# Blocks without tokens skipped and spread over the expert pairs, and all shared-expert units placed before the expert loop

## The chip, the cores and the metric

One core of one Trainium2 chip runs the whole kernel. The time is device microseconds of one execution, from the first to the last instruction; lower is better. TensorE (PE), VectorE (DVE), ScalarE (ACT), GpSimd (POOL) and SyncE (SP) each run their own instruction list in order and meet only at semaphores; SP, ACT and POOL also issue DMA transfers, each on a queue of its own (q1, q10 and q0 in the profile).

## The reference

Four layers on x of shape (8, 256, 256), each `x = x + layernorm(layer(layernorm(x)))`: softmax attention with 16 heads, a mixture of experts, an mLSTM layer with 8 heads, and a gated feed-forward layer with 2:4 sparsity. The change concerns the second:

```python
_, topk_idx = jax.lax.top_k(logits + router_bias, K)          # 64 experts, K = 4, 2048 tokens
combine = jnp.zeros((n, E), x.dtype).at[jnp.arange(n)[:, None], topk_idx].add(topk_scores)
g = jnp.einsum('nd,edf->enf', flat, Wg)
u = jnp.einsum('nd,edf->enf', flat, Wu)
h = jax.nn.silu(g) * u
out = jnp.einsum('enf,efd->nd', h * combine.T[:, :, None], Wd)
for i in range(Sg.shape[0]):                                  # 2 shared experts, 256 wide each
    sh = jax.nn.silu(flat @ Sg[i]) * (flat @ Su[i])
    out = out + sh @ Sd[i]
```

## The kernel before, in words

**Attention** (to about 290 us of the profile). For each of the 8 batches the normed input of the expert layer is stored to the DRAM tensor `xnd`, on SP's queue.

**Shared experts and router** (about 290 to 357 us). The two shared experts are cut into 16 units: unit n is token group n // 4 (512 tokens) and weight block n % 4. A unit is `gate(n)`, `up(n)` on PE (12 matmuls of 512 columns), a Silu on ACT (`hidden_gate`), a product on DVE, a rounded copy on ACT (`hidden_high`), the rest of it by a subtraction on POOL (`low_hidden`), and `down_unit(n)` on PE (12 matmuls of 256 columns), which PE issues two units later. After four units ACT copies the group's rows out (`shared_rows`) and SP stores them to `shd`. The constant `AHEAD` says how many units stand ahead of the expert loop: 12 of 16. Between them DVE computes the router's choice (`router_step(n)` after unit n's product): the number of blocks of 128 tokens that each expert needs, the table `ebrow` of the expert of each block, and the token numbers in each block, `rows_at`. For the last, DVE writes 0/1 marks for four token tiles at a time (`mark_rows(c)`, c = 0 to 3), ACT multiplies them by the token's number (`token_marks(c)`), PE contracts them (`block_rows(c)`, 16 matmuls), and DVE copies the sum out (semaphore `r_inv`).

**The expert loop** (about 357 to 580 us). There are always 128 blocks, in 64 pairs; pair i is blocks 2i and 2i+1. Tokens of one expert fill whole blocks and a partly filled last one; blocks behind the last used one have no tokens, and take expert 63. From the inputs and the reference's routing 96 blocks are used, with 8192 filled places in all, so that blocks 96 to 127, the pairs 48 to 63, are empty. For each pair:
- SP reads each block's expert number and loads its weights, 192 KB a block, into one of 7 slots (`expert_weights`).
- POOL issues two indirect gathers of token rows from `xnd` (L529) into one of 4 slots; a place without a token transfers nothing. It waits until PE has transposed pair i-4.
- PE transposes the rows (L1298), ACT copies them (L782), PE multiplies gate and up (L1310), ACT takes the Silu (L798), DVE the product (L1999), PE multiplies down (L1321), DVE copies the result (L2006), and ACT issues the store of 256 KB to `yd` (L787). PE's order is: transposes of i+1, gate and up of i, down of i-1.

During pairs 8 to 23 DVE also does one step each of the combine weights (`weight_step`).

**After the loop** PE runs the units 12 to 15. Meanwhile POOL waits for all stores of the loop and fetches batch 0's expert rows from `yd` (`gathers(0)`, 8 indirect gathers, L545), DVE sums them (L1962), adds, and norms twice (L1566); with that PE starts the mLSTM layer (L938). SP stores the last shared rows and then loads the first half of the feed-forward weights, 1.5 MB. The mLSTM layer and the feed-forward layer follow, to 1017.7 us.

Of the kernel before, what the change touches and what calls it, by code (L numbers as in the profile page):

```python
# [15 lines left out]
P = 128  # L16
# [10 lines left out]
NJ = NSH  # L27
NQ = NUNIT
AHEAD = (NQ - 1) * NJ
# [25 lines left out]
def build(nc, io, out):  # L55
    ctx = ExitStack()
    with ctx:
# [31 lines left out]
        ebrow = sb("ebrow", [1, XB], mybir.dt.int32)  # L89
# [202 lines left out]
        def sums(b):  # L292
# [17 lines left out]
            x_st r_zero r_oh r_im r_inv sh_o0 sh_o1 e_xt e_xc e_gu e_sg e_h e_dn e_y e_w0 e_w1 e_w2 e_w3 e_x0 e_x1 e_x2 e_x3  # L310
# [23 lines left out]
        def pair_weights(i):  # L334

            n = i % WRING
            return raw[:, n, :] if n < RING else more_weights[n - RING]

# [30 lines left out]
        def _(sp):  # L369
# [19 lines left out]
            for b in range(NB):  # L389
                sp.wait_ge(s["a_xn2"], b + 1)  # L390
                sp.dma_start(xnd[b * T:(b + 1) * T, :].rearrange("(t p) d -> p t d", p=P),
                             xn_all[:, 2 * b:2 * b + 2, :]).then_inc(s["x_st"], 16)

# [6 lines left out]
            def expert_weights(i):  # L400
# [11 lines left out]
            sp.wait_ge(s["r_eb"], 1)  # L412
            for i in range(RING):
                expert_weights(i)
# [26 lines left out]
        def _(pool):  # L441
# [83 lines left out]
            for i in range(XPAIR):  # L525
                if i >= RING:
                    pool.wait_ge(s["e_xt"], i - RING + 1)
                for b in range(2):
                    pool.indirect_dma_start(xg[:, i % RING, b, :], None, xnd[:],  # L529
                                            bass.IndirectOffsetOnAxis(ap=rows_at[:, 2 * i + b:2 * i + b + 1], axis=0),  # L530
                                            bounds_check=NT * P - 1, oob_is_err=False
                                            ).then_inc(s[f"e_x{i % RING}"], 16)
            for k in range(RING):
                pool.wait_ge(s[f"e_o{k}"], 16 * (XPAIR // RING))
# [45 lines left out]

            pool.wait_ge(s["r_w"], 1)
# [47 lines left out]
        def _(act):  # L629
# [132 lines left out]
            for n in range(1, AHEAD):  # L762
# [27 lines left out]
            act.wait_ge(s["r_inv"], 1)  # L790
            expert_inputs(0)
# [11 lines left out]

            for n in range(AHEAD, NQ * NJ):
                hidden_unit(n)
            shared_rows(3)
# [127 lines left out]
        def _(pe):  # L934
# [331 lines left out]
            for n in range(2, AHEAD):  # L1266
# [12 lines left out]
                if n == 11:  # L1279
                    block_rows(0)  # L1280
# [46 lines left out]
            pe.wait_ge(s["f_rows"], 2 * (NQ - 1))  # L1327
# [14 lines left out]
            for n in range(AHEAD, NQ * NJ):  # L1342
                gate(n)
                up(n)
                if n >= AHEAD + 2:
                    down_unit(n - 2)
            down_unit(NQ * NJ - 2)
            down_unit(NQ * NJ - 1)
            pe.wait_ge(s["f_rows"], 2 * NQ)
# [200 lines left out]
        def _(dve):  # L1550
# [326 lines left out]
            def block_table():  # L1877
                dve.wait_ge(s["r_ebT"], 1)
                dve.tensor_copy(ebrow[:], S[3][0:1, 0:XB]).then_inc(s["r_eb"], 1)
# [6 lines left out]
            def router_step(n):  # L1886
# [36 lines left out]
                if n == 11:  # L1923
                    for c in range(1, 4):
                        mark_rows(c)
# [67 lines left out]
            for i in range(XPAIR + 1):  # L1993
# [8 lines left out]
                if i:  # L2002
                    dve.wait_ge(s["e_dn"], i)
                    if i - 1 >= RING:
                        dve.wait_ge(s[f"e_o{(i - 1) % RING}"], 16 * ((i - 1) // RING))
# [7 lines left out]
            for n in range(AHEAD, NQ * NJ):  # L2013
                product(n)
# [326 lines left out]
```

## Time and profile before

| | |
|---|---|
| three timed runs, us | 979.53, 972.15, 970.7 (median 972.15) |
| profiled execution, span | 1017.7 us |
| PE busy | 862.2 us, 85% |
| DVE, ACT, POOL busy | 667.7, 389.5, 396.7 us |
| DMA | 77.66 MB, mean 76 GB/s |
| loads and stores | q1 (SP) 40.92 MB, q10 (ACT: the stores to `yd`) 16.78 MB, q0 (POOL) 18.92 MB |

The page gives the span and what each engine did in it. The span belongs to the one profiled execution, and is 45.5 us longer than the median of the timed runs. Idle time stands ahead of the instruction that had to wait, with the engine or transfer that released it; "issue" means that the profile shows nothing it waited for, "remote" and "another core or an unknown queue" that it shows no releaser.

### The profile page before, as it was taken

The page shows a single profiled execution, that of the slowest core. Times are in us where ns is not written, and L with a number is a line of the kernel's source. Part 1 is how long each engine was busy: PE and PEld are TensorE (multiplying, and loading weights), DVE is VectorE, ACT ScalarE, POOL GpSimd, SP SyncE. Part 2 cuts the span into 40 slices and gives each one's busy share as a digit, 9 for nine tenths or more (in the row PEclk, how much of TensorE's full clock was granted, in tenths as well). Part 3 has the DMA queues.
Part 4 walks back from the last instruction along what each step waited for, and adds up shares of the span by engine and source line. Part 5 has one row for each costly group of instructions (what it writes and reads, how often), then busy time and mean ns, then how long its engine had stood idle before and what let it go on. Part 6 is the DMA issues. An engine that isn't in the chain of part 4 may idle for free.

```text
span 1017.7 us, 18542 instructions
## 1 busy us (share of the span) xinstructions
PE 862.2 (85%) x6718; PEld 722.4 (71%) x6718; DVE 667.7 (66%) x1500; ACT 389.5 (38%) x764; POOL 396.7 (39%) x548
## 2 busy tenths in 40 slices
PE   4899899898688857667777859899999999999994
PEld 3777777776576846556666748778788888788883
DVE  6567777765577615885444547668778865867875
ACT  2244444444433713232222325435555564222220
POOL 3123333323432266766565283466665322100001
PEclk9799999998899968998898977758888887999997
DMA  7000000000000248888876551221111000000001
GB/s 248 2 1 13 12 12 9 5 12 12 22 1 22 87 136 260 250 257 242 242 222 184 162 178 52 82 59 52 46 42 41 0 1 1 0 1 21 22 1 41
DMA packets 59384, 77.66 MB, mean 76 GB/s; under 512 B 9746, under 2 KB 51997, under 8 KB 59304
## 3 DMA queue, kind: packets, MB, share of 16 engines
q1 hardware_dynamic: 32040, 40.92, 13.1%
q0 software_dynamic: 9856, 18.92, 6.9%
q10 hardware_dynamic: 17408, 16.78, 4.7%
q8 instruction: 47, 0.77, 0.3%
q14 instruction: 33, 0.27, 0.1%
HBM read 61.88 MB, written 23.07 MB: 83 GB/s over the span
## 4 chain that ended last, share of the span: by engine, by line
PE 43%; DVE 12%; issue 5%; another core or an unknown queue 4%; ACT 3%; POOL 2%; DMA 1%; ACTq 0%; POOLq 0%; DVEq 0%
PE S L1310 5%; PE S L1298 4%; PE S L959 3%; PE S L961 3%; PE S L960 3%; PE S L944 3%; PE ZO L1518 2%; PE ZO L1321 2%; PE T L1321 2%; PE T L1518 2%; PE ZO L1431 2%; DVE work L1566 1%; PE ZO L1433 1%; PE ZO L1432 1%
## 5 line engine op out<-in xcount | busy, mean ns | idle before, releaser
L529 POOL DMA_INDIRECT work<-xnd,rows_at x128 | 134.8, 1053 | 87.6 <-issue 38.6
L446 POOL TENSOR_SCALAR veps<-mv 128x2 f32<-128x2 f32 (+1 forms) x63 | 15.6, 247 | 287.8 <-DVE mv L1561 287.6
L1999 DVE TENSOR_TENSOR work<-work,S 64x256 f32<-64x256 f32 x128 | 54.2, 424 | 83.0 <-ACT work L798 52.9
L455 POOL TENSOR_SCALAR_AFFINE_SELECT work<-work 128x256 f32<-128x256 f32 x128 | 53.7, 444 | 118.0 <-ACT work L650 118.0
L959 PE MATMUL ZO<-parts 128*128 128x256 f32 x224 | 71.4, 319 | 16.6 <-DVE parts L1600 6.4
L959 PE MATMUL S<-xr,parts 128*128 128x512 f32 x192 | 83.5, 435 | 0.8 <-issue 0.8
L960 PE MATMUL S<-xr,parts 128*128 128x512 f32 x192 | 77.5, 404 | 0.0
L961 PE MATMUL S<-xr,parts 128*128 128x512 f32 x192 | 77.5, 403 | 0.0
L782 ACT ACTIVATE work<-S 128x512 f32<-128x512 f32 x64 | 38.2, 597 | 100.7 <-PE S L1298 43.5
L650 ACT ACTIVATE work<-S 128x768 f32<-128x768 f32 x64 | 51.7, 812 | 55.5 <-PE S L1033 55.5
L960 PE MATMUL ZO<-parts 128*128 128x256 f32 x224 | 66.3, 296 | 0.0
L961 PE MATMUL ZO<-parts 128*128 128x256 f32 x224 | 66.2, 295 | 0.0
L1033 PE MATMUL S<-parts 32*128 32x256 f32 (+1 forms) x768 | 57.9, 288 | 4.8 <-DVE parts L1626 3.8
L959 PEld LDWEIGHTS ZO<-parts 128*128 128x128 f32 x224 | 45.3, 202 | 21.9 <-issue 9.3
L1310 PE MATMUL S<-work,raw 128*128 128x128 f32 x296 | 46.7, 309 | 10.8 <-issue 10.7
L545 POOL DMA_INDIRECT attn_w<-yd,slots x44 | 49.8, 1131 | 11.9 <-issue 11.9
L1298 PE MATMUL S<-ident,work 128*128 128x128 f32 x256 | 47.4, 314 | 8.2 <-DMA work<-xnd,rows_at 8.2
L1033 PEld LDWEIGHTS S<-parts 32*128 32x128 f32 x768 | 48.9, 191 | 7.1 <-DVE parts L1626 5.0
L1310 PEld LDWEIGHTS S<-work,raw 128*128 128x128 f32 x296 | 42.5, 221 | 13.0 <-issue 12.9
L447 POOL TENSOR_TENSOR rstd<-veps,mhalf 128x2 f32<-128x2 f32 (+1 forms) x63 | 48.1, 763 | 5.2
L798 ACT ACTIVATE work<-S 64x256 f32<-64x256 f32 x64 | 24.1, 377 | 59.1 <-remote 30.8
L960 PEld LDWEIGHTS ZO<-parts 128*128 128x128 f32 x224 | 45.8, 205 | 0.1
(330 smaller groups left out, 2355.7 us busy)
## 6 DMA issues: line engine op xcount, KB each, us to landing
yd<-work ACTq DMA_DIRECT2D x64, 256.0 KB
raw<-in_experts SPq DMA_DIRECT2D x74, 192.0 KB
work<-in_experts SPq DMA_DIRECT2D x36, 192.0 KB
lg_all<-in_experts SPq DMA_DIRECT2D x18, 192.0 KB
xnd<-attn_w SPq DMA_DIRECT2D x8, 256.0 KB, 2.1
shd<-work SPq DMA_DIRECT2D x8, 256.0 KB, 2.3
work<-xnd,rows_at POOLq DMA_INDIRECT x128
raw<-in_ffn SPq DMA_DIRECT2D x2, 1024.0 KB, 5.4
```

The lines of the kernel that those rows point to most:

```text
L447: pool.tensor_tensor(rstd[:, 0:n], veps[:, 0:n], mhalf[:, 0:n], ALU.pow).then_inc(s["ln_rs"], 1)
L455: last = pool.affine_select(out=diagonal, in_=diagonal, compare_op=ALU.is_ge, fill=0.0, base=0, pattern=[[0, 2], [1, P]], channel_multipli ...
L529: pool.indirect_dma_start(xg[:, i % RING, b, :], None, xnd[:], bass.IndirectOffsetOnAxis(ap=rows_at[:, 2 * i + b:2 * i + b + 1], axis=0), ...
L545: pool.indirect_dma_start(gathered(b, t, k), None, yd[:], bass.IndirectOffsetOnAxis(ap=slots[:, 2 * b + t, k:k + 1], axis=0)).then_inc(s[" ...
L650: act.activation(pt[n % 6], SS[:, at:at + 1024].rearrange("p (r x) -> p r x", r=2)[:, :, 0:384], ACT.Exp).then_inc(s["a_exp"], 1)
L959: pe.matmul(dst, a(0), b(0), start=start, stop=False, skip_group_check=True)
L960: pe.matmul(dst, a(0), b(1), start=False, stop=False, skip_group_check=True)
L961: return pe.matmul(dst, a(1), b(0), start=False, stop=stop, skip_group_check=True)
L1033: return pe.matmul(bank[:, 2 * half * P:(2 + half) * P], side, top, start=k == 0 and half == 0, stop=k == 2, skip_group_check=True)
L1298: last = pe.transpose(S[i % 2][:, o:o + P], xg[:, i % RING, b, c * P:(c + 1) * P], ident[:])
L1310: last = pe.matmul(S[2 + i % 2][:, b * P:(b + 1) * P], pair_weights(i)[:, o:o + P], xT[:, i % 2, b, c, :], start=(c == 0), stop=(c == KC - 1))
L1999: last = dve.tensor_tensor(hx[64 * half:64 * half + 64, i % 2, :], sgx[64:128, i % 2, :], S[2 + i % 2][64:128, 0:256], ALU.mult)
```

## The change

1. Pair i is now blocks i and 64 + (27 i + 13) % 64 (`pair_blocks`). The first is always used; of the second ones 32 are empty, about every second pair.
2. SP's load of a second block's weights (from pair 7 on) and ACT's store of a second block carry a condition, `used > k`, and move nothing if the block is empty; the semaphore is still incremented. `used` is one more element of `ebrow`, read once by SP and once by ACT.
3. The store of a pair is two DMAs of 128 KB in place of one of 256 KB.
4. The upper 64 blocks of `yd` are filled beforehand with the input, 4 DRAM-to-DRAM copies of 2 MB each on SP's queue, behind the first four stores to `xnd` in the attention stage. ACT waits for them before the loop.
5. `AHEAD` is 16: all units stand ahead of the loop, none behind. `mark_rows`, `token_marks` and `block_rows` are spread over units 10 to 14.

```diff
-AHEAD = (NQ - 1) * NJ
+AHEAD = NQ * NJ
+        def pair_blocks(i):
+            return i, XPAIR + (27 * i + 13) % XPAIR
@@ SP
+                if b < 4:
+                    at = XPAIR * P + b * NT * P
+                    sp.dma_start(yd[at:at + NT * P, :], io["x"]).then_inc(s["y_base"], 16)
-                for b in range(2):
-                    e = sp.value_load(ebrow[0:1, 2 * i + b:2 * i + b + 1], min_val=0, max_val=E - 1)
-                    sp.dma_start(pair_weights(i)[:, b * EW:(b + 1) * EW],
-                                 io["experts"][bass.ds(e, 1)].squeeze(0)).then_inc(pair_loaded(i)[0], 16)
+                for b, k in enumerate(pair_blocks(i)):
+                    e = sp.value_load(ebrow[0:1, k:k + 1], min_val=0, max_val=E - 1)
+                    sp.dma_start(pair_weights(i)[:, b * EW:(b + 1) * EW], io["experts"][bass.ds(e, 1)].squeeze(0),
+                                 cond=used > k if b and i >= WRING else None).then_inc(pair_loaded(i)[0], 16)
+            shared_rows(3)
             for i in range(XPAIR):
                 if WRING <= i + WRING - 1 < XPAIR:
                     expert_weights(i + WRING - 1)
-            shared_rows(3)
@@ POOL
-                for b in range(2):
+                for b, k in enumerate(pair_blocks(i)):
                     pool.indirect_dma_start(xg[:, i % RING, b, :], None, xnd[:],
-                                            bass.IndirectOffsetOnAxis(ap=rows_at[:, 2 * i + b:2 * i + b + 1], axis=0),
+                                            bass.IndirectOffsetOnAxis(ap=rows_at[:, k:k + 1], axis=0),
@@ ACT
-                if n in (6, 10):
+                if n in (6, 10, 14):
                     shared_rows((n - 6) // 4)
-                if n == 10:
-                    token_marks(0)
-            for c in range(1, 4):
-                token_marks(c)
-            shared_rows(2)
+                if 10 <= n < 14:
+                    token_marks(n - 10)
+            shared_rows(3)
-                act.dma_start(yd[i * 256:(i + 1) * 256, :].rearrange("(b p) d -> p b d", p=P),
-                              ysb[:, i % RING].rearrange("p b h d -> p b (h d)")).then_inc(s[f"e_o{i % RING}"], 16)
+                for b, k in enumerate(pair_blocks(i)):
+                    act.dma_start(yd[k * P:(k + 1) * P, :], ysb[:, i % RING, b].rearrange("p h d -> p (h d)"),
+                                  cond=used > k if b else None).then_inc(s[f"e_o{i % RING}"], 16)
-            for n in range(AHEAD, NQ * NJ):
-                hidden_unit(n)
-            shared_rows(3)
@@ PE
-                if n == 11:
-                    block_rows(0)
+                if 11 <= n < 15:
+                    block_rows(n - 11)
                 if n >= 2:
                     down_unit(n - 2)
             down_unit(AHEAD - 2)
-            block_rows(1)
             down_unit(AHEAD - 1)
-            block_rows(2)
-            block_rows(3)
@@ DVE
-                if n == 11:
-                    for c in range(1, 4):
-                        mark_rows(c)
+                if 11 <= n < 14:
+                    mark_rows(n - 10)
+                if n == 14:
                     block_rows()
```

PE and DVE lose their loops `for n in range(AHEAD, NQ * NJ)` behind the expert loop in the same way.

**POOL, in front of the gathers.** `parts` is the output of `low_hidden`, `rows_at` the index table of the token gathers. Before:

```order
L466 TENSOR_TENSOR parts<-work,parts 128x512 [waits f_hh] x7
L521 MEMSET work 128x2048 [waits r_mask]
L466 TENSOR_TENSOR parts<-work,parts 128x512 [waits f_hh] x5
L529 DMA work<-xnd,rows_at 128x256 [waits r_inv,x_st,r_zero]
L529 DMA work<-xnd,rows_at 128x256 x7
```

Now:

```order
L474 TENSOR_TENSOR parts<-work,parts 128x512 [waits f_hh] x7
L529 MEMSET work 128x2048 [waits r_mask]
L474 TENSOR_TENSOR parts<-work,parts 128x512 [waits f_hh] x9
L537 DMA work<-xnd,rows_at 128x256 [waits r_inv,x_st,r_zero]
L537 DMA work<-xnd,rows_at 128x256 x7
```

Sixteen of these subtractions, unit 15's among them, stand in front of the first gather where twelve did.

**PE, at the end of the expert loop.** The L1321 rows are the down products of the last two pairs. Before, the first unit of the last token group follows at once (`xr`, `parts` into `S`):

```order
L1321 MATMUL T<-lg_all,work 128x128 [waits e_y,e_h]
L1321 MATMUL T<-lg_all,work 128x128 x3
L1321 MATMUL ZO<-raw,work 128x128 [waits e_y,e_h]
L1321 MATMUL ZO<-raw,work 128x128 x3
L959 MATMUL S<-xr,parts 128x512 [waits f_sg,e_y,e_h]
L960 MATMUL S<-xr,parts 128x512
```

Now the mLSTM layer's first transposes (L945, L938 before) and gate product do:

```order
L1325 MATMUL T<-lg_all,work 128x128 [waits e_y,e_h]
L1325 MATMUL T<-lg_all,work 128x128 x3
L1325 MATMUL ZO<-raw,work 128x128 [waits e_y,e_h]
L1325 MATMUL ZO<-raw,work 128x128 x3
L945 MATMUL T<-ident,work 128x128 [waits c_const,w_c,c_xn,e_y,e_h]
L945 MATMUL T<-ident,work 128x128 x3
L1356 MATMUL T<-work,attn_w 40x256 [waits c_xtc]
```

The 96 matmuls of units 12 to 15 are gone from this place, and the wait for the normed input (`c_xn`) is the next thing that PE meets.

## Rows read from the trace of the kernel before

**Rows 1.** The page: busy time of two engines; shares of the chain that ended last.
```profile
PE 862.2 (85%) x6718; PEld 722.4 (71%) x6718; DVE 667.7 (66%) x1500; ACT 389.5 (38%) x764; POOL 396.7 (39%) x548
...
PE 43%; DVE 12%; issue 5%; another core or an unknown queue 4%; ACT 3%; POOL 2%; DMA 1%; ACTq 0%; POOLq 0%; DVEq 0%
```

**Rows 2.** The chain that ended last, in time: start us, us, what.
```profile
390.81 2.02 another core or an unknown queue
...
550.70 4.24 another core or an unknown queue
```

**Rows 3.** Stretches: us, busy (instructions) of PE, PEld, DVE, ACT, POOL, PEclk, DMA share, GB/s.
```profile
140.00:180.00 40.00, 36.68 (x506) 29.67 (x508) 29.81 (x75) 18.02 (x36) 13.49 (x32) 1.00 0.04 15
...
436.00:456.00 20.00, 13.60 (x122) 11.31 (x122) 16.31 (x26) 5.80 (x13) 13.85 (x13) 1.00 0.84 258
...
519.80:524.00 4.20, 1.28 (x10) 0.97 (x8) 0.00 (x0) 0.51 (x1) 2.43 (x3) 1.00 0.42 126
```

**Rows 4.** Timeline of PE in front of the loop: start us, us, engine, line, instruction, [idle before].
```profile
332.89 0.40 PE L959 MATMUL S<-xr,parts 128*128 128x512 f32 x1
335.69 0.28 PE L959 MATMUL T<-parts 128*128 128x256 f32 x1
337.13 0.40 PE L959 MATMUL S<-xr,parts 128*128 128x512 f32 x1
...
342.26 2.06 PE L1204 MATMUL S<-work 128*128 128x128 f16 x16 [2.18 <-ACT work L757]
344.08 0.43 PE L959 MATMUL T<-parts 128*128 128x256 f32 x1
```

**Rows 5.** The same timeline, from the last `block_rows` to the first transposes.
```profile
354.51 2.06 PE L1204 MATMUL S<-work 128*128 128x128 f16 x16 [0.60 <-ACT work L757]
363.03 1.09 PE L1298 MATMUL S<-ident,work 128*128 128x128 f32 x4 [6.46 <-DMA work<-xnd,rows_at]
```

**Rows 6.** POOL: all `low_hidden` (min/median/max ns), and the first gather of the timeline.
```profile
L466 POOL TENSOR_TENSOR parts<-work,parts x12: 1262/1296/2841, 283.0 to 344.2; 128x512 fp32r<-128x512 f32 x12
```
```profile
357.90 1.29 POOL L529 DMA_INDIRECT work<-xnd,rows_at  x1 [12.20 <-DVE rows_at L1866]
```

**Rows 7.** The token gathers on POOL: duration ns, and what ended the idle time before them.
```profile
L529 POOL DMA_INDIRECT work<-xnd,rows_at x128: 996/1002/2380, 357.9 to 567.1; - x128
...
  issue: 38.6, 105
```

**Rows 8.** Timeline of DVE: copies of the results of pairs 12, 13, 25, 47, 48, 57, 63.
```profile
416.48 0.69 DVE L2006 COPY work<-T 128x512 f32<-128x512 f32 x1
...
419.35 0.69 DVE L2006 COPY work<-ZO 128x512 f32<-128x512 f32 x1
...
458.94 0.69 DVE L2006 COPY work<-ZO 128x512 f32<-128x512 f32 x1
...
534.31 0.69 DVE L2006 COPY work<-ZO 128x512 f32<-128x512 f32 x1 [0.23 <-remote]
...
536.29 0.69 DVE L2006 COPY work<-T 128x512 f32<-128x512 f32 x1
...
569.10 0.69 DVE L2006 COPY work<-ZO 128x512 f32<-128x512 f32 x1 [0.25 <-remote]
...
579.28 0.69 DVE L2006 COPY work<-ZO 128x512 f32<-128x512 f32 x1
```

**Rows 9.** Timelines behind the loop: PE, POOL, DVE, and SP's load of feed-forward weights.
```profile
596.99 0.28 PE L961 MATMUL ZO<-parts 128*128 128x256 f32 x1
...
607.04 1.09 PE L938 MATMUL T<-ident,work 128*128 128x128 f32 x4 [9.77 <-DVE work L1566]
```
```profile
582.83 0.77 POOL L558 DMA_DIRECT2D attn_w<-shd  x1 [14.68 <-issue]
```
```profile
596.37 3.63 DVE L1962 SCALAR_TENSOR_TENSOR attn_w<-attn_w,wtop 128x256 f32<-128x256 f32 x8 [1.25 <-DMA attn_w<-yd,slots]
```
```profile
602.93 0.50 SPq L430 DMA_DIRECT2D raw<-in_ffn  x1
```

More of the change, by code:

```diff
@@ L88, in build @@
         wtop = sb("wtop", [P, NT, TOPK])
-        ebrow = sb("ebrow", [1, XB], mybir.dt.int32)
+        ebrow = sb("ebrow", [1, XB + 1], mybir.dt.int32)
         eye1 = sb("eye1", [P, H1])
@@ L309, in build @@
             f_g f_u f_sg f_h f_hh f_hl f_wh f_wl f_blk f_rows
-            x_st r_zero r_oh r_im r_inv sh_o0 sh_o1 e_xt e_xc e_gu e_sg e_h e_dn e_y e_w0 e_w1 e_w2 e_w3 e_x0 e_x1 e_x2 e_x3
+            x_st y_base r_zero r_oh r_im r_inv sh_o0 sh_o1 e_xt e_xc e_gu e_sg e_h e_dn e_y e_w0 e_w1 e_w2 e_w3 e_x0 e_x1 e_x2 e_x3
             e_o0 e_o1 e_o2 e_o3 m_in m_in1 m_add
@@ L412, in _ @@
             sp.wait_ge(s["r_eb"], 1)
+            used = sp.value_load(ebrow[0:1, XB:XB + 1], min_val=0, max_val=XB)
             for i in range(RING):
@@ L533, in _ @@
             for k in range(RING):
-                pool.wait_ge(s[f"e_o{k}"], 16 * (XPAIR // RING))
+                pool.wait_ge(s[f"e_o{k}"], 32 * (XPAIR // RING))
             base = 3 * NB
@@ L578, in head_event @@
                 pool.tensor_tensor(hv, hv, mhalf[:], ALU.pow).then_inc(s["c_hr"], 1)
+            pool.wait_ge(s["y_base"], 64)
             pool.wait_ge(s["r_w"], 1)
@@ L786, in expert_rows @@
                 act.wait_ge(s["e_y"], i + 1)
-                act.dma_start(yd[i * 256:(i + 1) * 256, :].rearrange("(b p) d -> p b d", p=P),
-                              ysb[:, i % RING].rearrange("p b h d -> p b (h d)")).then_inc(s[f"e_o{i % RING}"], 16)
+                for b, k in enumerate(pair_blocks(i)):
+                    act.dma_start(yd[k * P:(k + 1) * P, :], ysb[:, i % RING, b].rearrange("p h d -> p (h d)"),
+                                  cond=used > k if b else None).then_inc(s[f"e_o{i % RING}"], 16)
             act.wait_ge(s["r_inv"], 1)
+            act.wait_ge(s["r_eb"], 1)
+            act.wait_ge(s["y_base"], 64)
+            used = act.value_load(ebrow[0:1, XB:XB + 1], min_val=0, max_val=XB)
             expert_inputs(0)
@@ L1325, in expert_down @@
                 last.then_inc(s["e_dn"], 1)
-            pe.wait_ge(s["f_rows"], 2 * (NQ - 1))
+            pe.wait_ge(s["f_rows"], 2 * NQ)
             pe.wait_ge(s["f_sg"], AHEAD)
@@ L1341, in _ @@
             pe.wait_ge(s["e_y"], XPAIR)
[L1342 to L1349, printed above, removed]
             pe.wait_ge(s["w_c"], 144)
@@ L1878, in block_table @@
                 dve.wait_ge(s["r_ebT"], 1)
-                dve.tensor_copy(ebrow[:], S[3][0:1, 0:XB]).then_inc(s["r_eb"], 1)
+                dve.tensor_copy(ebrow[0:1, XB:XB + 1], upto[0:1, E - 1:E])
+                dve.tensor_copy(ebrow[0:1, 0:XB], S[3][0:1, 0:XB]).then_inc(s["r_eb"], 1)
             def combine_weights():
@@ L2004, in _ @@
                     if i - 1 >= RING:
-                        dve.wait_ge(s[f"e_o{(i - 1) % RING}"], 16 * ((i - 1) // RING))
+                        dve.wait_ge(s[f"e_o{(i - 1) % RING}"], 32 * ((i - 1) // RING))
                     dve.tensor_copy(ysb[:, (i - 1) % RING].rearrange("p b h d -> p h b d"),
@@ L2012, in _ @@
                     second_constants(i - 24)
-            for n in range(AHEAD, NQ * NJ):
-                product(n)
-                dve.wait_ge(s["f_hh"], n + 1)
-                dve.tensor_tensor(hp[:, n % 4, 1, :], hf[n % 2], hp[:, n % 4, 0, :], ALU.subtract).then_inc(s["f_hl"], 1)
             moe_sum(0, ch)
```

## The prediction

> **What bounds the kernel now.** I read the page first, then the chain of waits in order of time, then stretches by engine, then the timelines of single engines around the three places that the change touches. PE is busy 85% of the span [rows 1], and the chain that ended last runs mostly over it. The exception is the expert loop: in a stretch of it PE works 13.60 of 20 us, POOL 13.85, and the DMA engines are 84% busy at 258 GB/s [rows 3]. From the first gather (357.90) [rows 6] to the end of the last result copy (579.28 + 0.69) [rows 8] it takes 222.1 us.
>
> Part of that is not in what I can explain. The chain of waits has pieces of 2.0 and some 4.3 us whose releaser the trace does not show [rows 2]; nine of them lie inside the loop, 29.5 us in all. In one of them PE works 1.28 of 4.2 us while the DMA engines carry 126 GB/s at a share of 0.42 [rows 3], half of what they carry elsewhere in the loop: they are not a matter of a full DMA. All such pieces are 4% of the span [rows 1], some 37 us, and the profiled execution is 45.5 us longer than the median. I take them for something that the timed runs have not, or have less of, and the loop as 222.1 - 29.5 = 192.6 us.
>
> What sets its pace: POOL issues two gathers of 1.002 us a pair, each behind 0.30 us of issue (38.6 us before 105 of them, with some longer ones) [rows 7], 2.61 us a pair, 64 x 2.61 = 167 us. In pairs 8 to 23 DVE's extra step makes it 2.87 us (416.48 to 419.35) [rows 8], + 16 x 0.26 = 4 us. The first gather has 5.1 us to the first transposes (357.90 [rows 6] to 363.03 [rows 5]); with that at the end, where the last pair still goes through, the floor is 176 us. The excess over it is 192.6 - 176 = 16.6 us.
>
> **The change part by part.** The sum goes against the profiled execution's own 1017.7 us and is carried over to the median 972.15, since no term of it stands in the unexplained pieces.
>
> *Four units ahead of the loop.* A unit takes PE 337.13 - 332.89 = 4.24 us, of which gate and up 2.80 and down 1.44 [rows 4]. In front of the loop PE is idle 2.18 us until the first marks (342.26), 0.60 before the last `block_rows`, and 6.46 before the first transposes [rows 4, 5]. Now PE is full from 342.26 on: 4 times `block_rows` at 2.0 (8.0), downs 9 to 12 (5.8, and 1.1 more because the first goes at half the clock, 0.43 us where 0.28 stands otherwise [rows 4]), gate and up of 12 to 15 (11.2) make 368.4 us. `rows_at` is ready before that (it needs `block_rows(3)`, at unit 14), but POOL's list has the `low_hidden` of unit 15 ahead of the gathers. Unit 15 needs DVE's product (0.7), ACT's copy (0.6), POOL's 1.3 [rows 6] and hops, about 0.5: first gather at 371.5, first transposes 5.1 us later at 376.6. Before it was 363.03: **+13.6 us**. Of the 17.0 us of the four units only the last downs hide, in the gather's latency. Queued behind that gather are all 128, and all engines wait for them.
>
> *The same units taken from behind the loop.* They ended at 597.3, then PE was idle 9.77 us until the normed input, 607.04 [rows 9]. That input does not come from them: stores landed, POOL starts at 582.83, its eight gathers land at 596.37, where DVE had been idle 1.25 us waiting for the DMA; then sum, norm, norm [rows 9]. From the last result copy to 607.04 it is 27.8 us with or without the units. **0 us**, and PE's idle time grows to 27 us. If the gathers had landed earlier in the timed runs, DVE would have been held by the units, which end only 1.25 us before: at most -1.3.
>
> *Feed-forward weights.* SP's load of 1.5 MB at 602.93 [rows 9] stood behind the shared rows of units 12 to 15; now it starts at the loop's end, beside the last stores and batch 0's gathers. At 258 GB/s [rows 3] it is 6 us of DMA; POOL's gathers ask 128 KB every 1.3 us, 100 GB/s, so both fit. 0 to +6, I take **+1**.
>
> *The loop.* Weights 25.2 MB, stores 16.8, token rows 8.4 make 50.4 MB. Skipped are 29 weight loads (5.7 MB; pairs 0 to 6 load both) and 32 stores (4.2 MB): 40.5 MB, 20% less, and evenly. But PE, ACT, DVE and POOL still do all 64 pairs: POOL issues 128 gathers, empty or not. So the floor of 176 stays, and only the excess of 16.6 can go. How much of it is DMA? Pairs 48 to 63 fetch no rows, and went 536.29 to 569.10, 9 pairs in 32.8 us, less one piece of 4.24 [rows 2] 3.2 us a pair; pairs 25 to 47, with full traffic, 22 in 75.4 (458.94 to 534.31) [rows 8], less three such pairs of pieces 2.6 us. Less payload did not make them faster. Against it stands a DMA share of 0.84, and 815 KB a pair in the first 48 now against 635 KB then. Bounds 0 and 16.6; I take half, **-8.3**.
>
> *ACT's second store.* At 0.37 us the issue, ACT goes from about 1.4 to 1.8 us a pair, under POOL's 2.61; only the last six pairs, which ran at 1.7 us (569.10 to 579.28) [rows 8], could feel it: 0 to +1, in the loop's term. No conditional DMA is in the trace; below, a skipped one costs nothing, above, as a full issue (0.37), and both hide under POOL.
>
> *The copies into `yd`.* 2 MB each in stretches where the DMA share is 0.04 [rows 3]; behind them on SP's queue are only stores to `xnd`, first read at 371 us. 0 us. Without that cover it would be 8 us each at 258 GB/s.
>
> Sum: 13.6 + 0 + 1 - 8.3 = +6.3: profile 1024, median 972.15 + 6.3 = **978.5 us**.
>
> **The rivals.**
> 1. *The loop does not shorten* (the pace is POOL and the ring of 4 slots, as pairs 48 to 57 say), and the weights' load costs 3: +16.6, 989 us. For it: rows 8. Chance 0.25.
> 2. *The DMA was the bound and the excess goes wholly*: 13.6 + 1 - 16.6 = -2, 970 us. The Trainium skill ("DMA: Bandwidth & Descriptors", section on latency and other measured facts) says that the access latency of the memory grows from 0.2 to 2 us at high load, so that lighter traffic makes each transfer's fixed cost smaller; by that rule this rival holds, and the trace's share of 0.84 agrees while pairs 48 to 57 don't. Chance 0.17.
> 3. *Faster*: the unexplained pieces are real, in the timed runs too, and come from the loop's traffic. If they go with it, 29.5 us [rows 2] less: the two DMA terms together -8.3 - 29.5, 949 us; if half go, 964. It decides when more than 16 us of them vanish. Against it: they come at a share of 0.42 as well [rows 3]. Chance 0.13.
> 4. *Nothing but the front*: skipping costs more than it saves, for instance ACT held by conditional stores above 2.61 us a pair. Each 0.1 us a pair more is 6 us: 995 or more. Chance 0.05.
>
> The rest, 0.40, is my forecast, with a range of its own from 974 to 984.
>
> **How the numbers follow.** Least is left out with 962 to 990: below it most of rival 3, above it rival 4 and a tail of rival 1. A measurement tells about 1% from no change, 962.4 and 981.9 here. Faster: rival 3 and a little of 2, 0.14. Slower: rivals 1 and 4, and the upper end of mine, 0.36. Same: 0.50.
>
> **What would show it.** In the profile after, the first transposes of the expert loop at 376 to 377 us with the last `low_hidden` just ahead of the first gather; then 64 pairs with POOL's gathers still 1.3 us apart; PE idle some 27 us between the last down product and the first mLSTM transposes, and that distance unchanged at 28 us. I am wrong if the loop, without unexplained pieces, is under 176 or over 195 us; if the first transposes come by 370; or if the stretch behind the loop shrinks.

## The result, and the profile after

| | before | after |
|---|---|---|
| timed runs, median us | 971.42 (970.15 to 979.53, 4 runs) | 985.24 (983.89 to 986.49, 4 runs) |
| ratio to before, 95% interval | | 1.0106 (1.0075 to 1.0138) |
| timed once more | 972.54 (17 runs) | 985.74 (6 runs); ratio 1.0132 (1.0101 to 1.0164) |
| profiled execution, span | 1017.7; a second one 975.1 (below) | 984.2 |

The change makes the kernel slower, by 10 us (1.06% of 971.42) to 13 us (1.32% of 972.54) as the two ratios have it; the medians of the first line are 13.8 us apart, with runs before that reach from 970.15 to 979.53. The forecast of 978.5 is 7 us too low, the range of 962 to 990 holds the result.

The page of after. First the shares of the chain that ended last, then three DMA queues (packets, MB, share), then the gathers' group (busy and mean ns, idle before):

```profile
PE 32%; DVE 14%; issue 9%; POOL 7%; DMA 4%; ACT 3%; ACTq 0%; POOLq 0%; DVEq 0%
...
q1 hardware_dynamic: 28056, 43.60, 13.8%
q0 software_dynamic: 9856, 18.92, 7.4%
q10 hardware_dynamic: 13824, 12.59, 3.8%
...
L537 POOL DMA_INDIRECT work<-xnd,rows_at x128 | 134.0, 1046 | 39.4 <-issue 31.9
```

The pieces "another core or an unknown queue" of [rows 1, 2] are gone. q10, the stores of the loop, has 12.59 MB; with nothing skipped it has 16.78 (the profile of the kernel before, taken again). The 4.19 MB of difference are 32 stores of 128 KB. All 128 gathers are still there.

**In front of the loop.** The timelines of POOL and PE, which answer to [rows 5, 6]:

```profile
369.26 1.30 POOL L474 TENSOR_TENSOR parts<-work,parts 128x512 fp32r<-128x512 f32 x1 [4.77 <-ACT parts L724]
370.74 1.29 POOL L537 DMA_INDIRECT work<-xnd,rows_at  x1 [0.18 <-issue]
```
```profile
375.58 1.09 PE L1302 MATMUL S<-ident,work 128*128 128x128 f32 x4 [3.28 <-DMA work<-xnd,rows_at]
```

Unit 15's `low_hidden` (its rounding rest, worked out on POOL) ends at 370.56 and the first gather follows in 0.18 us. The transposes start at 375.58 where they started at 363.03: 12.55 us later, against 13.6 forecast.

**The loop.** First and last issue of a gather on POOL (one line's instructions, durations in ns), and the copy of pair 63's result in DVE's timeline:

```profile
L537 POOL DMA_INDIRECT work<-xnd,rows_at x128: 994/998/2810, 370.7 to 542.9; - x128
```
```profile
551.33 0.69 DVE L2003 COPY work<-ZO 128x512 f32<-128x512 f32 x1
```

From the first gather to the end of that copy, 552.02, it is 181.3 us.

**Behind the loop.** Stretches of the loop and of what follows it (us, busy time of PE, PEld, DVE, ACT, POOL, clock, DMA share, GB/s), then the timelines of SP, POOL and PE, against [rows 9]:

```profile
370.70:552.00 181.30, 144.44 (x1292) 124.80 (x1292) 122.55 (x219) 63.30 (x130) 133.95 (x128) 0.97 0.75 217
552.00:583.00 31.00, 0.00 (x0) 0.01 (x1) 7.71 (x22) 1.28 (x1) 18.95 (x23) 0.50 0.46 140
```
```profile
551.32 0.39 SPq L438 DMA_DIRECT2D raw<-in_ffn  x1
```
```profile
559.40 0.77 POOL L566 DMA_DIRECT2D attn_w<-shd  x1 [15.54 <-issue]
```
```profile
583.02 1.09 PE L945 MATMUL T<-ident,work 128*128 128x128 f32 x4 [31.74 <-DVE work L1562]
```

PE has nothing to do for 31 us, and the granted clock is 0.50 there, the lower of its two levels (1.2 GHz). The stretch is 31.0 us; before it was 27.1 (607.04 - 579.97) [rows 8, 9]. The 4 us lie at its start: POOL fetches the first rows 7.4 us after the last copy (559.40 - 552.02), where it was 2.9 (582.83 - 579.97) [rows 8, 9]. By its list, what POOL waits for there is that all stores of the loop have landed.

### The profile page after: what moved, and what is told of

Same layout as the page of the kernel before. It is cut to its first block, busy times and chain, and to the rows that moved or that the text cites. A ratio compares the mean times of both kernels' runs of the same rounds, so it can differ in the third digit from the quotient of the medians.

```text
span 984.2 us, 18747 instructions
## 1 busy us (share of the span) xinstructions
PE 832.9 (85%) x6718; PEld 700.8 (71%) x6718; DVE 667.6 (68%) x1497; ACT 389.0 (40%) x764; POOL 400.6 (41%) x552
## 3 DMA queue, kind: packets, MB, share of 16 engines
q1 hardware_dynamic: 28056, 43.60, 13.8%
q10 hardware_dynamic: 13824, 12.59, 3.8%
## 4 chain that ended last, share of the span: by engine, by line
PE 32%; DVE 14%; issue 9%; POOL 7%; DMA 4%; ACT 3%; ACTq 0%; POOLq 0%; DVEq 0%
DMA work<-xnd,rows_at 4%; POOL work L537 3%; PE S L966 3%; PE S L968 3%; PE S L967 3%; PE S L951 3%; PE ZO L1514 2%; DVE work L1562 2%; DVE st L1554 2%; PE T L1514 2%; PE ZO L1427 1%; PE S L1302 1%; PE S L1314 1%; POOL attn_w L553 1%; PE ZO L1429 1%
## 5 line engine op out<-in xcount | busy, mean ns | idle before, releaser
L537 POOL DMA_INDIRECT work<-xnd,rows_at x128 | 134.0, 1046 | 39.4 <-issue 31.9
L789 ACT ACTIVATE work<-S 128x512 f32<-128x512 f32 x64 | 38.2, 597 | 96.6 <-PE S L1302 91.5
L1302 PE MATMUL S<-ident,work 128*128 128x128 f32 x256 | 43.3, 293 | 23.6 <-DMA work<-xnd,rows_at 23.2
L1302 PEld LDWEIGHTS S<-ident,work 128*128 128x128 f32 x256 | 27.7, 144 | 33.7 <-DMA work<-xnd,rows_at 26.1
L945 PE MATMUL T<-ident,work 128*128 128x128 f32 x96 | 19.5, 338 | 36.9 <-DVE work L1562 34.1
L474 POOL TENSOR_TENSOR parts<-work,parts 128x512 fp32r<-128x512 f32 x16 | 24.4, 1522 | 61.9 <-ACT parts L724 61.9
```

The costliest lines, as they stand in the source:

```text
L1302: last = pe.transpose(S[i % 2][:, o:o + P], xg[:, i % RING, b, c * P:(c + 1) * P], ident[:])
```

## The experiments

Each ratio is to the kernel before, timed in the same round (median 971.42 for after, 974.6 for e1 to e3, 974.54 for e4 to e7, 972.54 for e8 to e11), so that two rows are best compared by their ratios. The rest of this table is put together from the traces: first gather, last gather, end of the last result copy, POOL's fetch behind the loop, first mLSTM transposes. "Loop" is the third of these less the first, "stream" the second less the first, "stretch" the fifth less the third.

| kernel | median us | ratio (95%) | first gather | stream | loop | fetch after copy | stretch |
|---|---|---|---|---|---|---|---|
| e0_before_again | 977.2 (1 run) | | 359.31 | 171.3 | 184.3 | 2.9 | 27.3 |
| e1_skip_spread | 970.8 | 0.9962 (0.9924 to 0.9999) | 357.91 | 171.4 | 180.7 | 2.8 | 26.8 |
| e2_units_ahead | 991.4 | 1.0176 (1.0125 to 1.0227) | 374.35 | 170.6 | 180.0 | 7.6 | 31.3 |
| e3_ffn_later | 982.4 | 1.0072 (1.0048 to 1.0096) | 368.29 | 171.2 | 181.3 | 2.8 | 26.4 |
| e4_first_rows | 965.7 | 0.9936 (0.9894 to 0.9978) | 372.32 | 147.9 | 161.4 | 7.3 | 30.9 |
| e5_no_skip | 990.4 | 1.0179 (1.0123 to 1.0235) | 373.71 | 170.6 | 180.1 | 7.9 | 31.5 |
| e6_gathers_first | 982.9 | 1.0090 (1.0065 to 1.0115) | 366.27 | 172.4 | 181.2 | 7.4 | 31.1 |
| e7_gated | 954.1 | 0.9797 (0.9743 to 0.9852) | 360.71 | 150.7 | 163.4 | 4.6 | 28.2 |
| e8_after_again | 985.7 | 1.0132 (1.0101 to 1.0164) | 370.94 | 170.6 | 180.2 | 7.5 | 31.2 |
| e9_no_skip_again | 987.9 | 1.0164 (1.0125 to 1.0202) | 369.50 | 172.1 | 183.6 | 8.3 | 31.9 |
| e10_gated_weights_spread | 952.5 | 0.9789 (0.9742 to 0.9835) | 361.94 | 145.7 | 158.6 | 4.6 | 28.5 |
| e11_weights_spread | 973.0 | 0.9997 (0.9971 to 1.0022) | 359.55 | 171.8 | 181.8 | 2.9 | 27.3 |
| after | 985.2 | 1.0106 (1.0075 to 1.0138) | 370.74 | 172.1 | 181.3 | 7.4 | 31.0 |

### The parts of the change, one at a time

**The kernel before, profiled again**, no edit:

> The kernel before, unchanged, for a second profile. Theory A (the unexplained pieces of 2 and 4 us belong to that one profiled execution and not to the kernel): a span near 970 us, and from the first gather to the end of the last result copy of the loop 184 to 189 us in place of 222. Theory B (they are real and come from the loop's traffic): the pieces are there again, the loop takes 210 us or more and the span is over 1000 us.

Span 975.1 us. The chain's shares on its page:

```profile
PE 24%; DVE 11%; POOL 4%; issue 4%; ACT 1%; DMA 0%; POOLq 0%; DVEq 0%; ACTq 0%
```

These add up to 44%: the chain can be followed back no further than POOL's last three gathers, at 527.97, and so says nothing of the loop. What POOL's gathers waited for does, first in the trace that the prediction was made from, then in this one ("remote" is idle time without a releaser):

```profile
its engine sat idle before it (us, times) until:
  issue: 38.6, 105
  remote: 18.3, 9
  PE S L1298: 18.1, 12
```
```profile
its engine sat idle before it (us, times) until:
  issue: 34.6, 111
  DVE rows_at L1866: 12.2, 1
  PE S L1298: 4.6, 15
```

The gathers of one line, and the copy of pair 63:

```profile
L529 POOL DMA_INDIRECT work<-xnd,rows_at x128: 994/999/2017, 359.3 to 530.6; - x128
```
```profile
542.92 0.69 DVE L2006 COPY work<-ZO 128x512 f32<-128x512 f32 x1
```

Nothing "remote" is left, the loop is in theory A's 184 to 189 us, and the span of 975.1 is 5 above the 970 that A named and far from B's 1000: the unexplained pieces belonged to the one execution whose trace the prediction was made from. But the loop is 184.3 us (543.61 - 359.31), not the 192.6 that I had kept after taking 29.5 us of such pieces off.

**Skipping and spreading alone**: the changed kernel with its units back in their old places:

```diff
-AHEAD = NQ * NJ
+AHEAD = (NQ - 1) * NJ
```

> Parts 1 to 4 of the change alone: empty blocks skipped and spread, two stores a pair, the copies into yd; twelve units ahead of the loop and four behind it, as before. Theory A (the units' move costs 13 us in front of the loop and some 4 behind it, and the skipping gives back only 4 to 7 in the loop): loop 181 us, time 965 to 968 us against 971.4. Theory C (POOL's gathers and the ring of four slots set the pace, the traffic is hidden): 971 to 973 us. Theory D (the second store and the conditions cost more than is saved): above 974 us.

Ratio 0.9962: 3.7 us, at the edge of what can be told from nothing. The loop is 180.7 us, as theory A had it, but 970.8 us lies between its 965 to 968 and theory C's 971 to 973. Theory D, above 974, falls. The first gather comes at 357.91, where it came at 357.90 [rows 6] without the copies into `yd`.

**The units alone**, against the kernel before; nothing skipped, blocks 2i and 2i+1 paired as they were:

```diff
-AHEAD = (NQ - 1) * NJ
+AHEAD = NQ * NJ
...
-            for n in range(AHEAD, NQ * NJ):
-                hidden_unit(n)
-            shared_rows(3)
```

> Part 5 alone: all sixteen units ahead of the loop; no skipping, no spreading, one store of 256 KB a pair, no copies into yd. Theory A: first gather 13.3 us later, the stretch behind the loop 2 to 4 us longer, loop as before: 971.4 + 13.3 + 3 = 988 us (986 to 991). Rival: the place of the units is neutral, since PE works them either way, and the loss of the change comes from its DMA parts: 971 to 974 us.

1.0176, 991.4 us, just above theory A's 986 to 991; the rival, that the units' place is neutral, falls. The first gather comes at 374.35, the stretch behind the loop is 31.3 us and not 27. So both losses, in front and behind, come from moving the units, the one behind by way of the feed-forward load, which had stood behind their rows on SP's list (the next experiment). The loop with nothing skipped is 180.0 us, no longer than with skipping.

**The feed-forward weights held back** until batch 0's nine transfers have landed, in the changed kernel:

```diff
                 sp.wait_ge(s["e_dn"], XPAIR)
+                if not half:
+                    sp.wait_ge(s["m_in"], 16 * 9)
```

> The changed kernel with one wait more on SP: the load of the first 1.5 MB of feed-forward weights waits until batch 0's shared rows and eight expert gathers have landed. Theory A (that load stands in the way of the last stores and of batch 0's gathers): from the end of the last result copy to the first mLSTM transposes 27 to 28 us in place of 31.0, time 985.2 - 3.5 = 981.7 us. Rival (the stretch is longer because ACT issues six stores in 3.67 us behind the last copies where it issued three in 2.89): stretch 30 to 31 us, time 985 us.

SP's and POOL's timelines:

```profile
565.09 0.39 SPq L440 DMA_DIRECT2D raw<-in_ffn  x1
```
```profile
552.40 0.77 POOL L568 DMA_DIRECT2D attn_w<-shd  x1 [11.96 <-issue]
```

POOL fetches 2.8 us after the last copy again (549.59), not 7.4, and the stretch is 26.4 us. So the load beside the last stores costs the stretch 4.5 us at its start, and the rival, ACT's six stores behind the last copies, falls: they are there as before. What the load costs the whole kernel is less sure. On the timed runs the ratio falls from 1.0106 to 1.0072, 3.3 us, with intervals that overlap; and in the trace of e3_ffn_later all that follows the stretch takes 405.8 us, 4.6 more than the 401.2 in after, as much as the stretch gained.

### What sets the pace of the loop

In every kernel of the table with 128 gathers the stream from the first to the last takes 170.6 to 172.4 us: with and without skipping, with and without spreading, with twelve or sixteen units ahead. 127 distances of 1.30 us are 165.

**One gather a pair.** The second block's rows are left out of the computation:

```diff
                 for b, k in enumerate(pair_blocks(i)):
+                    if b:
+                        continue
                     pool.indirect_dma_start(xg[:, i % RING, b, :], None, xnd[:],
```

> The changed kernel with one of the two row gathers of every pair left out: the second block of a pair keeps the zeros of its buffer, so its rows are not computed (this part of the result is left out); weights, transposes, matmuls, copies and stores stay as they are. Theory A, GpSimd's issue of the gathers (1.3 us from one to the next, 2.61 us a pair) sets the pace of the block loop: with 1.3 us a pair GpSimd is no longer last, the next bound is TensorE (16.2 us busy in 20 us at 2.62 us a pair, so about 2.1 to 2.2 us a pair), the loop from the first gather to the end of the last copy falls from 181.3 to 145 to 155 us and the time from 985.2 to 948 to 962. Rival B, the pace is set by the loads of the weights (217 GB/s in the loop) and the ring of seven: the loop stays at 175 to 183 us and the time at 979 to 987.

The loop falls by 20 us to 161.4, the time to 965.7; theory A holds in its direction, its 145 to 155 us and 948 to 962 were too low, and rival B's 175 us or more are far. The edit takes the second blocks' rows off the DMA engines as well (4.2 MB); e7_gated below does not. POOL now waits for PE:

```profile
L539 POOL DMA_INDIRECT work<-xnd,rows_at x64: 994/997/1539, 372.3 to 520.2; - x64
its engine sat idle before it (us, times) until:
  PE S L1304: 82.8, 59
```

**Nothing skipped**, the pairing, the two stores and the copies of x kept:

```diff
-                                 cond=used > k if b and i >= WRING else None)
+                                 )
-                                  cond=used > k if b else None)
+                                  )
```

> The changed kernel with the conditions on the weight loads and on the stores taken away (nothing is skipped; the pairing of block i with a second block of the upper half, two stores a pair and the copies of x stay). Theory A, GpSimd's gathers set the pace: the 29 loads and 32 stores that come back cost nothing on the path, the loop stays within 3 us of 181.3 and the time within 3 us of 985.2 (ratio to the kernel before 1.008 to 1.014). Rival B, the skipping did save time in the loop, as in my forecast: the loop goes back to 186 us or more and the time to 990 or more.

The same 80 us of the loop, first in this kernel, then in after:

```profile
440.00:520.00 80.00, 66.21 (x608) 56.89 (x608) 57.00 (x108) 29.21 (x60) 61.62 (x61) 1.00 0.95 293
```
```profile
440.00:520.00 80.00, 67.13 (x620) 58.19 (x618) 57.53 (x108) 29.76 (x61) 61.67 (x61) 1.00 0.82 235
```

The DMA engines go from a share of 0.95 and 293 GB/s to 0.82 and 235, and POOL issues 61 gathers in both; PE does 608 matmuls in one and 620 in the other. The loop is 180.1 us without skipping. That is theory A's loop. The time, however, was 990.4 (ratio 1.0179), outside of what theory A allowed and in rival B's 990 or more. Since the traces showed no place for it, both kernels were run again as they are, side by side:

> The changed kernel as it is, timed and profiled once more as the partner of e9_no_skip_again. So far its ratio is 1.0106, and the same with the skipping taken out 1.0179 with intervals that nearly touch, while the loops of the two profiles are alike (181.3 and 180.1 us). Theory A (skipping is worth nothing; the difference of the medians is scatter): ratio 1.010 to 1.017, within 0.003 of the partner. Theory B (skipping is worth 5 to 7 us somewhere): ratio 1.009 to 1.013 and the partner 0.004 to 0.008 above it.

> As e5_no_skip: the changed kernel without the conditions, nothing skipped. Theory A: within 0.003 of the ratio of e8_after_again. Theory B: 0.004 to 0.008 above it, and then the trace has to show the place; by the first pair of profiles it can't be the loop (180.1 against 181.3 us), more likely the start of the loop or the stretch behind it.

1.0132 and 1.0164, 0.0032 apart, between what the two theories said. Taken together (1.0119 as the mean of 1.0106 and 1.0132, 1.0172 of 1.0179 and 1.0164) the skipping is worth 0.5%, 5 us, with intervals of ±0.3 to ±0.6% on each; e1_skip_spread says 3.7 us. In the traces the loops with skipping and 128 gathers are 180.2 to 181.3 us (five traces), without 180.0 to 184.3 (five). The two longest, e0_before_again and e9_no_skip_again, got so near their end: from the last gather's issue to the end of the last copy they took 13.0 and 11.5 us, the other eight 8.9 to 10.1. Shortly before or in that piece PE waited over 2 us for one gather to land, and then the granted clock was lower, 0.87 in the piece itself in the first and 0.91 in the 20 us before it in the second. PE's wait and the piece in e0_before_again, then the piece in e5_no_skip, where nothing is skipped either:

```profile
533.91 1.12 PE L1298 MATMUL S<-ident,work 128*128 128x128 f32 x4 [2.22 <-DMA work<-xnd,rows_at]
```
```profile
530.58:543.61 13.03, 9.36 (x77) 7.95 (x75) 6.84 (x13) 2.90 (x7) 0.99 (x1) 0.87 0.37 121
```
```profile
544.29:553.84 9.55, 8.10 (x79) 6.87 (x78) 7.50 (x14) 3.19 (x7) 1.00 (x1) 1.00 0.42 140
```

So the loop itself shows no gain from skipping: 180.0, 180.1 and 181.8 us without it where that did not happen. Half a us stands in the stretch behind it (31.3, 31.5 and 31.9 against 31.0 to 31.2, with sixteen units ahead and the load in its place). The timed runs say some 4 to 5 us in all; where the rest lies stays open.

**The gathers of pairs 0 and 1 ahead of unit 15's `low_hidden`:**

```diff
+                if i == AHEAD - 1:
+                    pool.wait_ge(s["r_inv"], 1)
+                    gather_pair(0)
+                    gather_pair(1)
                 low_hidden(i)
...
-            for i in range(XPAIR):
+            for i in range(2, XPAIR):
```

> The changed kernel with the four gathers of pairs 0 and 1 issued by GpSimd ahead of the low part of the last shared unit (where GpSimd waits 4.77 us for ScalarE), nothing left out. Theory A, the loop is one stream of gathers on GpSimd, so that what starts it earlier ends it earlier: the first gather comes at 365 to 366 us instead of 370.7, GpSimd's four gathers take 5.2 us of which 4.8 lay idle, the last unit moves by under 1 us, the whole loop ends 3 to 5 us earlier, time 980 to 983. Rival B, TensorE's last shared unit (its matmuls at 366 to 375 us) or the weights set the end: the first gather is earlier but the last copy is not, time 984 to 987.

PE's timeline shows the first transposes:

```profile
375.71 1.09 PE L1308 MATMUL S<-ident,work 128*128 128x128 f32 x8 [1.18 <-ACT work L762]
```

They wait for ACT, no longer for the gather, and start no earlier than in after (375.58). The stream starts 4.5 us earlier (366.27) and the last copy ends 4.6 us earlier (547.47 against 552.02). So the end of the loop follows the start of POOL's stream and not PE's. The rows with 128 gathers say the same: the first gather moves from 357.9 to 374.4 us, and the loop stays at 180.0 to 184.3. The timed ratio of 1.0090, 982.9 us, is 1.6 us under after's first ratio and 4.1 under its second; with these intervals it fits the 3 to 5 us of theory A but does not prove them.

### Kernels that beat both

**The gathers of empty blocks not issued**, on e1_skip_spread:

```diff
+                        with pool.If(used > k):
+                            gather()
...
-                pe.wait_ge(s[f"e_x{i % RING}"], 32 * (i // RING + 1))
+                arrived[i % RING] = pe.snap(arrived[i % RING] + (pair_used > pair_blocks(i)[1]) * 16 + 16)
+                pe.wait_ge(s[f"e_x{i % RING}"], arrived[i % RING])
```

> The kernel before with the skipping and the spreading (twelve shared units ahead of the loop, as e1_skip_spread), and the gather of an empty second block not issued at all: GpSimd branches over it, and TensorE counts in a register how many gathers it has to wait for. Nothing is left out of the result. 32 of the 128 gathers go. Theory A, GpSimd's issue sets the pace: 32 x 1.3 = 42 us of issue go, the branches give back 64 x 0.1 to 0.3 us = 6 to 19 us, pace 2.1 to 2.3 us a pair where TensorE is then the bound, the loop falls from 180.7 to 148 to 162 us, time 938 to 955 (ratio 0.965 to 0.982). Rival B, a branch costs a refill of instructions or TensorE's register work delays its matmuls: the loop stays above 175 us, time 965 or more. Rival C, the loads of the weights are next: loop 165 to 175 us, time 955 to 965.

954.1 us, ratio 0.9797, and by the ratios 16 us less than e1_skip_spread. The time is in theory A's 938 to 955, the loop of 163.4 us is 1.4 above its 148 to 162; rivals B and C fall. POOL's timeline, one line of the gathers, and the 80 us of above:

```profile
461.26 1.00 POOL L540 DMA_INDIRECT work<-xnd,rows_at  x1 [0.30 <-issue]
462.91 0.99 POOL L540 DMA_INDIRECT work<-xnd,rows_at  x1 [0.65 <-issue]
465.04 1.00 POOL L540 DMA_INDIRECT work<-xnd,rows_at  x1 [1.14 <-PE S L1323]
```
```profile
L540 POOL DMA_INDIRECT work<-xnd,rows_at x96: 992/998/1579, 360.7 to 511.4; - x96
```
```profile
440.00:520.00 80.00, 76.50 (x717) 67.21 (x715) 57.19 (x116) 35.05 (x72) 47.15 (x47) 1.00 0.87 256
```

A gather behind a branch that passes one over comes 0.65 us after the last instead of 0.30: the branch costs 0.35 us and saves 1.30. PE does 717 matmuls in 80 us instead of 620, and it does so at 256 GB/s, above the 235 at which it waited in after. Of the 42 us of issue that went, the loop gained 17: the 32 branches took back 11, and POOL now waited 24.3 us for PE, where it had waited 4.0 in e1_skip_spread. That VectorE (pairs 8 to 23) and then TensorE bound the loop is read from their busy times, and tried in part below. Behind this loop POOL's fetch comes 4.6 us after the last copy, not 2.8, though the weights' load comes later; why stays open.

**VectorE's steps spread** over every second pair, in that kernel and in the kernel before:

```diff
-                if 8 <= i < 24:
-                    weight_step(i - 8)
+                if 8 <= i < 40 and i % 2 == 0:
+                    weight_step((i - 8) // 2)
```

> As e7_gated, with the sixteen steps that work out the routing weights on VectorE done at every second pair from pair 8 to 38 instead of at every pair from 8 to 23, and the constants' steps at pairs 40 to 43. Nothing is left out. Theory A, in pairs 8 to 23 VectorE is the bound of the loop (19.2 us busy in 20 us, 3.0 us a pair, alike in every kernel measured) and behind them TensorE (2.1 us a pair): with half the extra work per pair VectorE needs 1.6 + 0.6 = 2.2 us a pair, the eight pairs 9 to 16 take 17 to 19 us instead of 24.3, pairs 17 to 32 take 36 to 38 instead of 40.0, the loop falls from 163.4 to 152 to 157 us and the time from 954 to 943 to 949. Rival B, what is taken from pairs 8 to 23 comes back in pairs 24 to 39, because each step of 1.23 us stops TensorE for its whole length: loop 160 us or more, time 951 or more.

> The kernel before with only the steps of the routing weights at every second pair, nothing left out. Theory A: VectorE bounds pairs 8 to 23 at 3.0 us a pair, GpSimd's gathers the rest at 2.61; spread, VectorE needs 2.2 us and GpSimd bounds all pairs, so 16 x (3.04 - 2.61) = 7 us go, the loop falls from 184.3 to 174 to 179 us, time 965 to 970, ratio 0.991 to 0.996. Rival B, the loads of the weights of before (263 GB/s, 0.85 of the queues' time) hold the loop as well: the gain is under 3 us, ratio 0.997 or more.

In pairs 8 to 23 VectorE, busy 38.25 of 40 us from 400 us on in the last line below, does bind for the moment: in after the copies of pairs 8 and 16 are 24.3 us apart (409.73 and 434.04), 3.04 us a pair. Where POOL sets the pace it gives this back: the copies of pairs 24 and 32 are 17.2 us apart (456.88 and 474.09), 2.15 us a pair, because gathers had gone ahead into the four slots. So e11_weights_spread gains nothing (0.9997), and theory A's 7 us were wrong. Rival B's number came, but not its reason, since the loop is as long with and without the skipped loads: a stretch slower than the pace costs only what the slots in front of it can't hold, here POOL's 3.7 to 7.1 us of waiting for PE in all. In e10_gated_weights_spread the loop does get shorter, 163.4 to 158.6, but the ratio of 0.9789 can't be told from 0.9797. 158.6 and 952.5 are outside of theory A's 152 to 157 and 943 to 949; rival B has the time (951 or more) but not the loop (160 or more). Its stretches before and from 440 us, then e7_gated's before 440:

```profile
400.00:440.00 40.00, 38.20 (x352) 32.87 (x352) 37.95 (x64) 17.53 (x36) 28.69 (x28) 1.00 0.89 271
```
```profile
440.00:520.00 80.00, 72.35 (x663) 62.09 (x661) 61.66 (x117) 31.53 (x65) 41.21 (x42) 1.00 0.81 241
```
```profile
400.00:440.00 40.00, 30.16 (x278) 25.80 (x277) 38.25 (x58) 13.54 (x28) 21.56 (x22) 1.00 0.77 229
```

Up to 440 us PE does 352 matmuls instead of 278, behind it 663 instead of 717: what the spreading won first it gave back in part.

## Why the prediction was right and wrong

**The front: right.** +13.6 was forecast from PE's work in the marks and units and one gather behind unit 15. First gather forecast 371.5, measured 370.74; first transposes 376.6 and 375.58. Over the runs with twelve units ahead and the list of POOL as it was (four traces: e0, e1, e11, and 357.90 in [rows 6]) the first gather is at 358.7 in the mean, with sixteen (after, e2, e3, e5, e8, e9) at 371.3: 12.6 us. The six lie between 368.3 and 374.4, a scatter that a single trace does not show.

**Units gone from behind the loop: right as a term, 0.** They were hidden, by the way of batch 0's rows through POOL, DVE and the norms, as argued: with the load out of the way the stretch is 26.4 us without them (e3_ffn_later) and 26.8 to 27.3 with them (e0, e1, e11).

**The feed-forward load: mis-sized**, +1 against +4. I asked whether the queues had room for it (258 GB/s, and POOL asks 100) and took a mean rate. What counts is what is last: POOL waits for the last of 96 stores of 128 KB. In after, SP issues the load at 551.32, 0.7 us ahead of the end of the last copy. e3_ffn_later takes that away alone and the 4.5 us go; how the load holds the stores back no trace here shows. So the sign that the stretch stays at 28 us did not come: counted from the start of that copy, as the prediction did, it is 31.7. The upper bound of the term, +6, held it.

**The loop: mis-sized**, -8.3 against -3 in one pair of traces (184.3 to 181.3), about 0 in the traces without a late gather near the end (180.0 to 181.8 without skipping, 180.2 to 181.3 with it), and by the timed runs 4 to 5 us for all that the skipping does anywhere. The failing step is the excess, "192.6 - 176 = 16.6 us", and both of its ends are off. For the 192.6 I took off only the pieces that the chain of waits named, and they were not the whole of the disturbance: the same kernel without it needs 184.3, and without the late gather near its end 180 to 182. For the 176, the stream of the gathers was right (167 + 4 = 171 forecast, 170.6 to 172.4 measured), but I put 5.1 us behind it, and from the last issue to the end of the last copy it is 8.9 us or more; the shortest loop with 128 gathers is 180.0. So there was hardly an excess of which the skipping could take half. The hint was in the prediction itself: pairs 48 to 57 fetched no rows and went no faster; I weighed it against a DMA share of 0.84, and the share was the weaker witness. (Of the payload a pair beside it, 815 KB should be some 830; nothing hangs on it.)

**The second store and the copies into `yd`: right, 0.** q1 carries 8.4 MB more in front (and 5.7 MB of weights less: 40.92 before, 43.60 now), PE's busy time in 100 to 200 us is 91.5 us in both traces, and e1_skip_spread, which has the copies, starts its gathers when the kernel before does. ACT's issues stayed under POOL's pace.

**The rivals.** Rival 1, that the loop does not shorten because POOL and its slots set the pace, is what the runs show as mechanism; its 16.6 us were 3 too many against the medians' 13.8 (the front costs 12.6 and not 13.6, the load 4 and not 3, and some 4 to 5 us are saved by the timed runs). It should have had more than 0.25. Rival 2 needs the DMA to be the bound: at 293 and 235 GB/s the loop is as long. The rule of the Trainium skill behind it ("DMA: Bandwidth & Descriptors", section "Latency and other measured facts": lighter load on the memory makes a transfer's fixed cost smaller) may hold for the single transfer; here it would not shorten the stream, in which POOL waited for PE only 3.7 to 7.1 us, and no loop got shorter by it. The same section gives about 1 us to the first byte of a transfer from GpSimd, and puts it down to the software that writes its descriptors; no trace here shows a first byte, but GpSimd is busy for a median of 998 ns a gather, which fits, and a gather of an empty block, which moves nothing, takes as long (the shortest of 128 is 994). Rival 3 falls with e0_before_again, rival 4 with e1_skip_spread, which is no slower than the kernel before.

Adding up two traces, e0_before_again to after: front +11.4, loop -3.0, stretch +3.7, all behind it -3.0 (404.2 us from the mLSTM transposes to the end, then 401.2), together +9.1, which is the difference of the spans, 984.2 - 975.1. The last term is scatter: over the kernels of the table that part takes 399.4 to 404.2 us in no order that the edits explain (405.8 in e3_ffn_later, whose load comes later). The loop's -3.0 is +0.9 in the stream and -3.9 behind the last gather, where e0_before_again had its late gather; it is not the skipping's.

The forecast of +6.3 was half of the medians' 13.8: the loop's term was too good by 4 to 5 us, the load's too small by 3, the front's too large by 1. That the range held owes more to its 28 us, which took in rivals 1 and 2 as well, than to the sum. 985.2 lies outside of the 974 to 984 that the forecast gave itself, nearer to rival 1's 989, and beyond the 981.9 up to which I had called it no change, the outcome to which I gave the larger chance.

## What to carry to other kernels

Skipping the bytes of an empty item is worth little while the instruction that asks for them is still issued: find the engine whose issue sets the pace (here 128 gathers at 1.3 us) and skip there. The times of a profiled execution with stalls that the timed runs don't have can't be put right by taking off the pieces that are named; profile the kernel once more before a term is built on what is left over. And a large load placed next to the last small stores of a phase can delay whoever waits for the last of them, by 4.5 us here, with bandwidth free in the mean (140 GB/s over the stretch, where the loop had reached 293).

## What the hardware showed that was not expected

- An indirect gather of an empty block, whose 128 places are all without a token, costs GpSimd the same 1.00 + 0.30 us as a full one.
- A 1.5 MB load issued 0.7 us before the last copy ended delayed the landing of the last stores by 4.5 us (from 2.8 to 7.4 us after that copy), though the DMA share over the stretch was 0.46.
- A branch over one gather costs GpSimd 0.35 us (0.65 between gathers instead of 0.30). What the count kept in a register for TensorE's waits costs was not separated; with it PE was busy 76.50 of 80 us.
- One execution of the same program ran 42.6 us longer (1017.7 against 975.1 us of span), 37.8 of it in the loop (222.1 against 184.3).
